# A transformer block of attention and product-key experts: set-up work moved between engines, one gather split over two queues, the last batch's two halves exchanged, all orders rewritten

## The reference

```python
xn = (x - mean) / sqrt(var + 1e-5)
# attention: 16 heads of 8, rotary embedding on Q and K, causal softmax
scores = where(causal, Q @ K.T / sqrt(8), min);  att = softmax(scores) @ V @ Wproj
# ffn: a gated MLP plus experts by product keys (4 retrieval heads, 64 x 64 keys, 8 of 64 candidates each)
sim = q_parts @ keys;  sx, sy = top8(each half);  s, idx = top8(sx[:, None] + sy[None, :])
w   = silu(xn . down_embed[idx]) * softmax(s);  experts = sum(w * up_embed[idx])
mlp = silu(xn @ Wg + bg) * (xn @ Wu + bu) @ Wd + bd
```

## Time and profile before

| | |
|---|---|
| median of 3 runs | 814.54 us (814.17 to 816.74) |
| the profiled execution: own time | 816.29 us |
| its span, first to last instruction | 814.5 us |
| busy: PE, DVE, ACT, POOL | 689.5, 606.2, 532.5, 429.1 us |
| mean granted TensorE clock | 0.943 |

### The profile page before, as it was taken

How to read it: one execution, slowest core, us unless ns; L and a number is a source line. 1 busy time by engine, 2 the same in 40 slices (tenths; PEclk the granted TensorE clock), 3 DMA queues, 4 the chain that set the end, 5 groups by cost and what they waited for, 6 DMA issues and landing times.

```text
span 814.5 us, 15271 instructions
## 1 busy us (share of the span) xinstructions
PE 689.5 (85%) x5756; PEld 283.2 (35%) x5756; DVE 606.2 (74%) x1274; ACT 532.5 (65%) x811; POOL 429.1 (53%) x574
## 2 busy tenths in 40 slices
PE   0946678988788999995999889993898899998996
PEld 0613224333232344532443234432332244432322
DVE  1237999989989995794998995992798996693300
ACT  0611377381879868634899859743479968739992
POOL 8652299551899841374675742765135842245100
PEclk9985699998999899997999999998899999999999
DMA  5153300350200000035300000005420000000000
GB/s 135 54 74 53 57 2 3 62 80 4 39 1 4 1 1 2 27 62 94 56 2 4 2 1 27 2 27 74 55 31 5 1 2 1 27 13 4 2 1 14
DMA packets 33815, 22.48 MB, mean 28 GB/s; under 512 B 6381, under 2 KB 33389, under 8 KB 33741
## 3 DMA queue, kind: packets, MB, share of 16 engines
q1 hardware_dynamic: 33740, 21.51, 15.4%
HBM read 6.23 MB, written 2.10 MB: 10 GB/s over the span
## 4 chain that ended last, share of the span: by engine, by line
PE 41%; DVE 23%; ACT 11%; issue 8%; POOL 8%; SPq 4%; DMA 2%; POOLq 0%; ACTq 0%; DVEq 0%
DVE pmax L1049 13%; PE ybank L1280 9%; PE banks L1333 7%; PE banks L1312 6%; ACT pT L929 6%; DVE wsum L1117 6%; PE banks L1228 5%; PE banks L1257 5%; SPq L657 4%; DMA qs<-parts 2%; POOL xin L749 2%; PE banks L1238 2%; PE banks L1319 2%; PE banks L1266 1%; PE banks L1302 1%
## 5 line engine op out<-in xcount | busy, mean ns | idle before, releaser
L1049 DVE TENSOR_REDUCE pmax<-banks 128x2 f32<-128x1024 f32 (+3 forms) x304 | 344.4, 1159 | 74.1 <-PE banks L1238 60.3
L929 ACT ACTIVATE pT<-banks 128x1024 f32<-128x1024 f32 (+3 forms) x384 | 296.6, 818 | 64.1 <-PE banks L1266 45.2
L814 POOL TENSOR_TENSOR ssum<-sim 128x512 f32<-128x512 f32 x128 | 146.5, 1151 | 73.3 <-DVE wsum L1117 48.0
L1228 PE MATMUL banks<-ks,qs 48*128 48x512 bf16 (+3 forms) x768 | 119.2, 353 | 62.0 <-DMA qs<-parts 27.9
L1280 PE MATMUL ybank<-pT,vaug 128*32 128x512 f32 (+3 forms) x1536 | 166.0, 510 | 0.0
L1257 PE MATMUL banks<-qs,ks 51*128 51x512 bf16 (+3 forms) x768 | 123.4, 337 | 23.9 <-ACT pT L929 16.0
L1117 DVE SCALAR_TENSOR_TENSOR wsum<-ssum,best,wsum 128x512 f32<-128x512 f32 x128 | 128.3, 1011 | 8.6 <-ACT wsum L972 8.4
L972 ACT ACTIVATE wsum<-ssum,wbias 128x512 f32<-128x512 f32 x128 | 92.0, 730 | 29.9 <-POOL ssum L814 24.7
L831 POOL TENSOR_TENSOR coef<-coef,wsum 128x512 f32<-128x512 f32 x64 | 83.9, 1310 | 30.8 <-DVE wsum L1117 29.8
L1228 PEld LDWEIGHTS banks<-ks,qs 48*128 48x128 bf16 x768 | 33.8, 98 | 170.5 <-issue 73.8
L827 POOL TENSOR_TENSOR coef<-wsum 128x512 f32<-128x512 f32 x32 | 42.0, 1314 | 90.3 <-PE banks L1319 59.2
(11 more groups left out here) (110 smaller groups left out, 818.5 us busy)
## 6 DMA issues: line engine op xcount, KB each, us to landing
ks<-parts SPq DMA_DIRECT2D x96, 64.0 KB
qs<-parts SPq DMA_DIRECT2D x96, 64.0 KB
xin<-in_L_attn_x SPq DMA_DIRECT2D x4, 512.0 KB, 4.0
osb<-in_L_attn_x SPq DMA_DIRECT2D x8, 256.0 KB, 2.8
out<-osb SPq DMA_DIRECT2D x8, 256.0 KB, 2.3
qs<-negmaxT SPq DMA_DIRECT2D x16, 24.0 KB
pT<-in_L_ffn_Wq SPq DMA_DIRECT2D x2, 128.0 KB, 3.3
pT<-in_L_ffn_down_embed SPq DMA_DIRECT2D x1, 256.0 KB, 3.5
```

What stands on the lines that cost most here:

```text
L814: g.tensor_tensor(ssum[:, m % NSS, :, :], s[:, h, 0:XI].unsqueeze(2).to_broadcast([P, XI, NKEYS]), s[:, RH + h:RH + h + 1, :].to_broadcast ...
L929: a_.activation(pT[:, q % NPT, 2 * e:2 * e + 2, q0:CHUNK], pair(("sc", *n))[:, :, q0:CHUNK], ACT.Exp, scale=SCALE).then_inc(out_sem, 1)
L1049: v.tensor_reduce(pmax[:, c, i % TPC, k0 // CHUNK, :].rearrange("p (e j) -> p e j", e=2) [:, :, js[0]:js[-1] + 1], pair(("mx", b, c, k))[: ...
L1228: ins = t_.matmul(bank[:, e, s * wd_:(s + 1) * wd_], qs[r, serial(b, c) % NQS, j, i % TPC * P:(i % TPC + 1) * P], ks[r, b % 2, j, k0:k0 + ...
```

## The change

1. **Set-up.** The 12 selects that make `id2`, `mask2`, `maskT2` become a POOL task `mc`, first in POOL's list, which only `mx` waits for; the small constants before them are fewer. `va` comes after `rs.0`. `rw` goes from POOL to ACT (8 copies of 128x256). The addition of EPS goes from POOL to DVE. For batch 0, the normalization goes from POOL to DVE (`xv`), and for the first two units (0,0,1) and (0,0,0) `ro`, `r1`, `p2` go from POOL to DVE (`rv`, `v1`, `v2`). PE does `rt.0`, `rt.1` ahead of `xt.0`, then `qk.0.0.1` at once; `vm.0` is later.
2. **Two queues.** Of the 12 copies of each of these two units, 6 (the upper half of the partitions) are issued by ACT (task `gq`), 6 by SP.
3. **Last batch.** The stages of batch 3 are done in the order 3.1, 3.0. `serial`, `tile`, `unit_at` and the modular buffer numbers follow this.
4. **Orders.** All five lists are new. Among much else: in batch 3, `qk.3.1.1`, `qk.3.1.0`, `qk.3.0.1` stand ahead of the last attention of stage 2.1; in batch 2, `qk.2.*` stands further ahead of `mx.2.0.0`; the units `mx.3.0.*` stand between the attention steps of 3.1; the experts of tiles 3.4 to 3.7 and then 3.0 to 3.3 come in the last quarter.

```diff
+STAGES = [(b, c) for b in range(B) for c in (range(NC) if b < B - 1 else reversed(range(NC)))]
 def serial(b, c):
-    return NC * b + c
+    return SERIAL[b, c]
...
                     for t, term in enumerate(TERMS):
-                        for hh in range(2):
+                        for hh in range(2 if m > 0 else 1):
...
-                if kind == "rw":
+                if kind == "mc":
+                    for k in range(4):
...
-                    k = mark(g.tensor_tensor(vareps[:, :], meanvar[:, :, 1], eps[:, :], ALU.add))
-                    need(k)
...
+                elif kind == "gq":
+                    b, c, a = n
+                    w.wait_ge(done["v2"], rank("v2", b, c, a))
+                    for t, term in enumerate(TERMS):
+                        r = HALF + DH * t
+                        dst = ks[r:r + DH, b % 2, :, 0:CHUNK] if a else qs[r:r + DH, 0, :, :]
+                        act.dma_start(dst, parts[HALF:P, a, term[a], :]).then_inc(rows_loaded[a], 16)
+                elif kind == "rw":
+                    s, i = n
+                    w.wait_ge(first_loaded, 16 * NFIRST)
+                    for e in range(2):
+                        ins = a_.activation(rope_wide[:, NT * s + 4 * i:NT * s + 4 * i + 4, e, :, :],
+                                            rope_sb[:, s, 4 * i:4 * i + 4, :].unsqueeze(3)
+                                            .to_broadcast([P, 4, DH, PAIRS]), ACT.Copy)
...
+                elif kind == "xv":
+                    w.wait_ge(done["rs"], rank("rs", b))
+                    for m in (2 * i, 2 * i + 1):
+                        ins = v.tensor_scalar(xin[:, m, :], xin[:, m, :], meanvar[:, m, 0:1], rstd[:, m:m + 1],
+                                              ALU.subtract, ALU.mult)
+                elif kind == "rv":
+                    v.tensor_tensor(tAB[:, a, 0, :], tAB[:, a, 0, :], tAB[:, a, 1, :], ALU.add).then_inc(out_sem, 1)
+                elif kind == "v1":
+                    v.tensor_tensor(tAB[:, a, 0, :], tAB[:, a, 0, :], parts[:, a, 0, :], ALU.subtract)\
+                elif kind == "v2":
+                    v.tensor_tensor(parts[:, a, 2, :], tAB[:, a, 0, :], parts[:, a, 1, :], ALU.subtract)\
...
-xt.0@01 rt.0@23 vm.0@01 rt.1@23 qk.0.0.1@01 qk.0.0.0@23 su.0@45 gt.0.0.0@6 su.1@01 dn.0.0.0@5 dn.0.0.1@4 dn.0.0.2@6
+rt.0@01 rt.1@23 xt.0@01 qk.0.0.1@01 qk.0.0.0@23 su.0@01 su.1@45 gt.0.0.3@6 gt.0.0.0@3 su.2@01 qk.0.1.1@45 dn.0.0.0@6
...
-(POOL) va rs.0 xn.0.0 xn.0.1 xn.0.2 xn.0.3 rw.0.0 rw.0.1 rw.1.0 rw.1.1 rs.1
+(POOL) mc rs.0 va rs.1 ro.0.1.1 xn.1.0 xn.1.3 ro.0.1.0
+(ACT) rw.0.0 rw.0.1 rw.1.1 rw.1.0 Rt.0 Rt.1 Xt.0 c0.0.0.1 Su.0 Su.1 c1.0.0.1 c0.0.0.0 Sg.0.0.3 c1.0.0.0 gq.0.0.1 gq.0.0.0
+(DVE) st.0 wp.1 wp.0 xv.0.2 xv.0.3 xv.0.0 xv.0.1 rp.0.0.1 rv.0.0.1 rp.0.0.0 v1.0.0.1 rv.0.0.0 v2.0.0.1 v1.0.0.0 st.1
```

More of the change, by code:

```diff
@@ L76 @@
[L76 to L80, removed]
@@ L432, with tile, tile_at @@
         _held.update((k, _t) for k in PLACE[_t])
+STAGES = [(b, c) for b in range(B) for c in (range(NC) if b < B - 1 else reversed(range(NC)))]
+SERIAL = {bc: m for m, bc in enumerate(STAGES)}
 def serial(b, c):
-    return NC * b + c
+    return SERIAL[b, c]
+def tile(b, i):
+    return TPC * serial(b, i // TPC) + i % TPC
+def tile_at(n):
+    b, c = STAGES[n // TPC]
+    return b, c * TPC + n % TPC
 def unit(b, c, a):
@@ L642, in _ @@
                     u = unit(b, c, a)
-                    w.wait_ge(done["p2"], rank("p2", b, c, a))
+                    if u < 2:
+                        w.wait_ge(done["v2"], rank("v2", b, c, a))
+                    else:
+                        w.wait_ge(done["p2"], rank("p2", b, c, a))
                     m = serial(b, c)
@@ L902, in _ @@
                     s = u % 2
-                    if kind == "c0":
+                    if kind == "c0" and u < 2:
+                        w.wait_ge(done["rv"], rank("rv", b, c, a))
+                    elif kind == "c0":
                         w.wait_ge(done["ro"], rank("ro", b, c, a))
@@ L990, in _ @@
                     if serial(b, c) > 0:
[L991 removed]
+                        w.wait_ge(done["ot"], rank("ot", *STAGES[serial(b, c) - 1]))
                     a_.activation(oT[:, :], single(("ac", b, c, 0)), ACT.Identity, bias=bd_sb[:, 0:1])\
@@ L1069, in _ @@
                     if serial(b, c) > 0:
-                        w.wait_ge(done["yo"], rank("yo", *divmod(serial(b, c) - 1, NC)))
+                        w.wait_ge(done["yo"], rank("yo", *STAGES[serial(b, c) - 1]))
                     wv = single(("yt", b, c, gr)).rearrange("p (n j d) -> p n j d", n=TPC, j=4)
@@ L1195, in _ @@
                     for i in range(4):
-                        w.wait_ge(done["xn"], rank("xn", b, i))
+                        if b == 0:
+                            w.wait_ge(done["xv"], rank("xv", b, i))
+                        else:
+                            w.wait_ge(done["xn"], rank("xn", b, i))
                     for m in range(NT):
```

768 lines of the change are left out of this document (398 added, 370 removed), and 3 rows, old and new, of the table KINDS.

## The result

| | before | changed |
|---|---|---|
| median | 815.64 us (814.17 to 817.69, 4 runs) | 770.80 us (767.23 to 772.61, 4 runs) |
| the profiled execution: own time, span | 816.29, 814.5 us | 770.97, 769.2 us |
| busy PE, DVE, ACT, POOL | 689.5, 606.2, 532.5, 429.1 us | 688.9, 613.1, 539.0, 414.4 us |
| mean granted TensorE clock | 0.943 | 0.953 |

The ratio is 0.9439, 95% interval 0.9407 to 0.9471: 45 us faster. A second set of runs gave 770.49 us, ratio 0.9431 (0.9391 to 0.9471). TensorE's busy time is the same to 0.6 us and its idle time went from 125.0 to 80.3 us: 44.7 of the 45.3 us between the spans.

The account below looks back on a forecast made before the run. The prediction took TensorE's 125 us of idle time as what could move the end. From 816.29, terms of -16.7, -7.4, -14.2, -2, -2 and +3.2 gave 777.2, less 1.75 for the median 775.4, called 775; range 758 to 796.

Parts of the forecast that it names:

- likeliest case: Whole kernel: the forecast itself, 775 us, with its own range 765 to 785; chance 0.63.
- Term 1: Start: first copy issued at 23.5 instead of 40.18 us, first maxima at 46.8 instead of 63.49; -16.7 us.
- The gather: First two gathers: DMA engines bound them, the second queue is worth nothing; 23.3 us again from first issue to first use.
- The first rival: First gathers: two queues do raise the copy rate, first maxima at 41.2 instead of 46.8, total 769 us; chance 0.13.
- Term 2: Batch 2, before the first maxima: more other TensorE work covers the wait for the gathers; -7.4 us.
- Term 3: Batch 3, before its first maxima: some 75 us of other work covers the gathers and the stall goes; -14.2 us.
- Term 4: After the stalls of batches 2 and 3: two starts of TensorE at a low granted clock are saved; -2 us.
- Term 5: End: 3.0's maxima fill idle time in 3.1's attention (-4), more work behind the last `pv` (+2); -2 us.
- Term 6: ScalarE: 37 table loads instead of 32, half of their cost exposed; +3.2 us, between 0 and 6.4.
- VectorE as the bound up to stage 1.1: Rival, up to stage 1.1: some 6 us more VectorE work in a window 7.4 us shorter, +13, 788 us; chance 0.14.
- The serial tail: Rival, last batch: the experts' 32 heads run serially behind the attention of 2.1, total 820 us; chance 0.04.
- Batch 3's gather: Rival, batch 3: key copies wait for `parts` buffers, the gather stays exposed, all of term 3 returns, 789 us; chance 0.06.

Follow-up runs that it names:

- both edits: The changed kernel with GpSimd's memsets held behind the first normalizations and `nr.1.1` issued ahead of stage 2.1's key copies: 758.57 us, ratio 0.9304.
- both edits and one queue: The changed kernel with those memsets held, `nr.1.1` moved ahead, and the first two gathers issued by SP alone: 759.86 us, ratio 0.9304.

## Why the prediction was right, and where it was not

Forecast 775, measured 770.8, inside the likeliest case's own range. Faster by far more than the 0.3% that a measurement can tell. That the total is so near is in part luck: by the three parts above the errors are +0.7, +7.9 and -14.8 us. (The prediction gives its sum as 775.4 and in one place as 774.5, from which its rivals' 769, 788 and 789 start; the terms add up to 775.4. And SP issues the two first gathers in 16.1 us, not 15.7. Neither matters to the argument.) Term by term:

- **Term 1, the start (-16.7): right.** The first maximum came 16.0 us earlier, and 17.1 us were kept to the end of stage 1.1 with the set-up alone in the profile; its median says 13.5. The working had errors that cancelled. `xv` at 0.2 us each is near what VectorE needs (2.14 for the eight) but not what it took (4.05), since I had set no price on `va`, which the change puts beside it. The product and its rotary step took 3.8 us instead of the 2.0 that I had read at a granted clock of 1.00. The power, 0.9 us earlier than I had it, and the transposes of x, 1.12 us instead of 2.0, gave part of that back. And from the first issue to the first maximum it took 2.5 us less where I had no change.
- **The gather.** The choice, the DMA engines are the bound and not the issue, was right: 2.1 us from the first issue on, nothing in the end that the spread lets one see, not 8. That half the DMA share means a fixed rate was not: see the last section. The first rival (769) is so excluded, though the time fell nearer to it.
- **Term 2, batch 2's wait (-7.4): the wait was right, its worth wrong.** The cover did suffice and the wait ahead of `mx.2.0.0` went. What failed is that I had asked what stands behind the moved gathers on SP for the start, but not here: `nr.1.1`, which the scores of stage 1.1 wait for. The old list has the same 12 key copies in front of it, but there its data came only when SP was nearly free, and the gathers before were less dense. The new place cost 4.56 us and the clock behind it. With the two tasks exchanged 6 us come. The rest of the middle part's error is mostly work that the new lists do before the cut (46 more products, 4.8 us).
- **Term 3, batch 3's wait (-14.2): right by itself.** The wait is gone in the changed kernel, and nothing was late next. Its size is no measure of what a gather moved by hand brings: in the old order the same 14 us went too, but 6 us of new waits and 6.7 us of work came elsewhere, and 7 us were left. What I missed is beside it: behind the end of stage 1.1 the changed kernel wins 30.1 us in the profile, and my terms for that part had 15.3. TensorE's idle time there falls from 36.3 to 12.6 us: 14.2 is this wait, 3.8 the end (below), and the other 6 are small waits in stages 2.0 to 3.1, which no term of mine had: those for exponentials outside the old last attention (3.3 us) and for single steps of the negated maxima and the rotary products (2.0 us) are mostly gone, those for a maximum to be taken are not (3.3 us before, 4.4 now).
- **Term 4, the clock (-2): not where I had it, and too small.** TensorE's busy time behind the cut falls by 6.3 us, at a granted clock of 1.00 instead of 0.97, with 24 of 2592 products fewer (about 3 us at the mean of that stretch). So some 3 us there, by this estimate, where I had 1; in batch 2 none was won until the new wait went.
- **Term 5, the end (-2): right in sign.** Idle time in the last attention falls from 7.34 to 3.97 us over both halves (I had 4), and the end behind it is not 2 us longer but the same (13.63 and 13.58): together -3.4 us, and 3.8 of TensorE's idle time.
- **Term 6, five more table loads (+3.2).** They are there. That they cost nothing fits the profile, whose total is explained without them, but no run took them out: it stays open.
- **The other rivals.** VectorE as the bound up to stage 1.1 (788) did not decide the time, but it is visible, and it may have a part in the +0.8 us of the middle: TensorE's waits for a maximum to be taken rose from 23.7 to 31.1 us over the whole run. The serial tail did not come. Batch 3's gather was covered.

The reason for the late part's full gain is settled only in part. Shown: it sits behind the end of stage 1.1; it doesn't depend on the order before, if the seam is paid; the gather's wait is under half of it (14.2 of 30.1 us). Not tried: the exchange of the two halves alone, which would need all five lists of the last batch written anew. That 3.0's maxima fill the attention of 3.1 is argued from the windows (0.06 us of idle time in the last 41.6 us of attention, 7.34 in 87.1 before).

## What to carry to other kernels

A big gather that many steps wait for and two small copies that one step waits for often share a queue: when gathers move forward and closer together, list what stands behind them, above all the small copies, see when the data of those are ready, and let them go first. That the order of two tasks has not changed is no answer: their times have. When work is moved onto an idle engine, look at what its neighbour does in the same microseconds, not only at its own row's price. And price a reordering by the idle time of the whole stretch behind it, not by its largest wait: here that wait was 14 of 30 us, and moving its copies ahead by hand, with nothing else rearranged, gave 7.

## What the runs showed that I had not expected

The same 24 copies do not always take the same time. In most profiles (before, changed, one queue, both edits) the first gathers moved at 63 to 99 GB/s for most of their time; in the one of the kernel with the later memsets, at up to 180 GB/s, with nearly the same share of the DMA engines. The same six microseconds of that kernel and of the changed one, inside the gathers in both:

```profile
30.00:36.00 6.00, 4.68 (x11) 1.94 (x12) 1.22 (x1) 2.04 (x4) 6.00 (x8) 1.00 0.53 170
```

```profile
30.00:36.00 6.00, 4.68 (x11) 1.74 (x10) 2.68 (x3) 0.00 (x0) 6.00 (x6) 1.00 0.57 79
```

With both edits and one queue it was 97 to 108 GB/s from 30 to 40 us, at a share of 0.41 to 0.44. So the share of the DMA engines does not tell the rate, and a packet takes about half the time in some executions. Why is open. A first maximum's time from one profile can be 4 us off by it, which is why I went by the medians for that edit.
